# Second gather of a graph kernel: one comparison of 1024 columns for four tiles' one-hots, followed by four additions, in place of one comparison per tile

## What is computed

```python
def _L1_gnn_ref(x, edge_index, W1, b1, W2, b2, gamma, beta):
    src, dst = (edge_index[0], edge_index[1])
    msg_sum = jax.ops.segment_sum(x[src], dst, num_segments=N)
    cnt = jax.ops.segment_sum(jnp.ones_like(dst, dtype=x.dtype), dst, num_segments=N)
    local_mean = msg_sum / jnp.maximum(cnt, 1.0)[:, None]
    feature_diff = jnp.tanh(jnp.linalg.norm(x - local_mean, axis=1, keepdims=True))
    enhanced = jax.nn.relu(x @ W1 + b1) @ W2 + b2
    h = x + ALPHA * enhanced * feature_diff
    ...
x = _layernorm(x + _L0_gnn_ref(...), axis=-1)
x = _layernorm(x + _L1_gnn_ref(x, edge_index, ...), axis=-1)
```

## Time and profile before

| | |
|---|---|
| median of 3 runs | 3951.27 us (3940.12 to 3954.78) |
| the profiled execution | 3949.06 us, its span 3947.3 us |
| busy over the span | PE 77%, DVE 75%, POOL 68%, ACT 56% |
| second gather, first product to last addition | 3044.0 to 3868.3 us |
| line 1461, DVE comparisons | 880, mean 361 ns |
| line 1453, DVE additions | 880, mean 424 ns |
| line 1258, POOL gathers of direct groups | 608, mean 959 ns |

### The profile page before, as it was taken

How to read it: one execution, slowest core, us unless ns; L and a number is a source line. 1 busy time by engine, 2 the same in 40 slices (tenths; PEclk the granted TensorE clock), 3 DMA queues, 4 the chain that set the end, 5 groups by cost and what they waited for, 6 DMA issues and landing times. The chain is left out here.

```text
span 3947.3 us, 81199 instructions
## 1 busy us (share of the span) xinstructions
PE 3027.4 (77%) x17192; PEld 2107.0 (53%) x17193; DVE 2949.3 (75%) x7793; ACT 2222.9 (56%) x6111; POOL 2695.6 (68%) x2634
## 2 busy tenths in 40 slices
PE   6865888888888999999999966767774477666652
PEld 2321444444436777777777745556663355455541
DVE  8998899989985555455454538999996589778857
ACT  1422999999985666666666659989993000000003
POOL 3887777777776777777777740048888777777770
PEclk8976999999999999999999987888887788888876
DMA  7332333333335888888888894457763222222232
GB/s 202 117 101 88 105 97 104 98 104 100 102 98 176 263 261 263 261 260 262 263 259 263 261 243 177 186 209 274 267 241 121 86 74 79 79 78 78 73 50 38
DMA packets 314706, 637.18 MB, mean 161 GB/s; under 512 B 54382, under 2 KB 188567, under 8 KB 306551
## 3 DMA queue, kind: packets, MB, share of 16 engines
q0 software_dynamic: 99440, 246.26, 22.6%
q1 hardware_dynamic: 172984, 266.56, 21.0%
q10 hardware_dynamic: 42192, 123.38, 8.3%
HBM read 423.94 MB, written 212.05 MB: 161 GB/s over the span
## 5 line engine op out<-in xcount | busy, mean ns | idle before, releaser
L367 POOL DMA_INDIRECT rec_d<-arena x830 | 886.0, 1068 | 311.2 <-issue 310.9
L853 POOL DMA_INDIRECT arena<-b_tab,arena x880 | 838.6, 953 | 292.1 <-issue 257.9
L767 PE MATMUL psum<-arena 128*128 128x440 f16 x3360 | 675.7, 356 | 34.9 <-ACT arena L461 33.3
L874 DVE TENSOR_TENSOR arena<-psum,arena 128x512 f32<-128x512 f32 x440 | 284.6, 686 | 551.5 <-DMA arena<-b_tab,arena 310.2
L964 PE MATMUL psum<-weT,arena 128*128 128x256 f32 x1760 | 548.7, 394 | 55.7 <-DVE arena L874 52.1
L461 ACT ACTIVATE arena<-arena 128x128 f16<-128x128 f16 x1680 | 561.7, 386 | 0.0
L626 DVE TENSOR_SCALAR arena<-iota_t,arena 128x880 f16<-128x880 f16 x840 | 500.8, 661 | 51.9 <-PE psum L767 49.3
L767 PEld LDWEIGHTS psum<-arena 128*128 128x128 f16 x3360 | 323.5, 99 | 381.9 <-DVE arena L626 56.3
L1453 DVE TENSOR_TENSOR arena<-psum,arena 128x256 f32 x880 | 372.9, 424 | 156.9 <-PE psum L1573 150.1
L1573 PE MATMUL psum<-x_sb,arena 128*128 128x256 f32 x1152 | 320.9, 439 | 198.7 <-DVE x_sb L1461 85.3
L967 PE MATMUL psum<-arena 128*128 x2640 | 435.1, 274 | 0.0
(11 more groups left out here) (255 smaller groups left out, 5807.2 us busy)
## 6 DMA issues: line engine op xcount, KB each, us to landing
z_d<-arena ACTq DMA_DIRECT2D x220, 512.0 KB
arena<-z_d SPq DMA_DIRECT2D x44, 2560.0 KB
arena<-rec_d SPq DMA_DIRECT2D x220, 260.0 KB
arena<-in_edge_attr SPq DMA_DIRECT2D x83, 640.0 KB, 4.8
arena<-early_d SPq DMA_DIRECT2D x34, 512.0 KB
arena<-b_tab,arena POOLq DMA_INDIRECT x880
rec_d<-arena POOLq DMA_INDIRECT x831, 3.4
early_d<-arena POOLq DMA_DIRECT2D x9, 1024.0 KB, 4.2
```

The source lines that it names most:

```text
L367: nc.gpsimd.indirect_dma_start(rec_rows, bass.IndirectOffsetOnAxis(e_idx[:, s, k:k + 1], 0), e_buf[:, s, k, :], None).then_inc(s_es[s], 16)
L767: last = nc.tensor.matmul(bank(4 + 2 * k + h)[:, 0:HALF], hot_lane[:, s, k, :], hot_tile[:, s, h * HALF:(h + 1) * HALF], start=start, stop ...
L853: nc.gpsimd.indirect_dma_start(bg[:, s, k, :], None, b_tab, bass.IndirectOffsetOnAxis(rec[:, s, k, H:H + 1].bitcast(I32), 0)).then_inc(s_b ...
```

## The change

The eight comparisons of 256 columns of a turn become two of 1024 columns, a `tensor_tensor` instead of a `tensor_scalar`. The ramp is repeated over four tiles, and the four columns of `l1_loc` are each repeated over 256 columns. The first stands ahead of additions 0 to 3, the second ahead of additions 4 to 7.

```diff
+        HOTS_IN_ONE = 4
...
                     wait(dve, s_sg, 8 * u - 8)
                     for k in range(G):
-                        t = first_tile(kind, n) + k
-                        last = nc.vector.tensor_scalar(hotg[:, place % 2, k, :], iota256[:], l1_loc[:, bass.ds(t, 1)], None, ALU.is_equal)
+                        if k % HOTS_IN_ONE == 0:
+                            t = first_tile(kind, n) + k
+                            wanted = l1_loc[:, bass.ds(t, HOTS_IN_ONE)].unsqueeze(2).broadcast_to([P, HOTS_IN_ONE, Z])
+                            last = nc.vector.tensor_tensor(hotg[:, place % 2, k:k + HOTS_IN_ONE, :], iota256[:].unsqueeze(1).broadcast_to([P, HOTS_IN_ONE, Z]),
+                                                           wanted, ALU.is_equal)
+                            if k + HOTS_IN_ONE == G:
+                                last.then_inc(s_hg, 1)
                         if before is not None:
-                            if k == G - 1:
-                                last.then_inc(s_hg, 1)
                             pair_add(*before[0:2], k, pairs[k])
-                    if before is None:
-                        last.then_inc(s_hg, 1)
```

## The result

The changed kernel takes 4049.35 us (median of 4 runs, 4046.95 to 4051.69) against 3945.69 us (4 runs, 3939.13 to 3954.78): 1.0254 times as long, with a 95% interval of 1.0238 to 1.027. That is 104 us slower by the medians; 4057 us was forecast. The profiled execution took 4049.35 us.

The account below looks back on a forecast made before the run. POOL's gathers were taken to bound the kernel, 20.3 us per three turns. Gathers held by the new comparisons add 108 us, VectorE's longer turn not added: 3949 + 108 = 4057 us; range 3998 to 4115, own range 4030 to 4085.

Parts of the forecast that it names:

- The comparison's price: VectorE's new 1024-column comparison: 1.22 us each, with the fifth addition starting 1.48 us after the fourth.
- rival 2: The new comparison's repeated operand reads slowly, up to 2.46 us each; 300 us at that bound, 4153 us halfway; chance 0.12.
- The comparison was free before: In VectorE's turns, the old short comparison filled a gap between additions 0.65 us apart, so its 318 us cost nothing.
- Gathers are held and set the pace: POOL's line 1258 gathers starting during a two-SBUF-input comparison are held until 0.83 us after it; mean 0.96 to 1.13 us.
- By chance: Hold on POOL's gathers priced by random hits: 0.45 us for each of 212 comparisons, 95 us.
- by alignment: Hold on POOL's gathers priced by where holding places later ones: 72 us loop, 36 unrolled, 7 last eight turns; together 115.
- the 108 us: The loss taken for held gathers over the whole kernel, chosen between 95 and 115 us, nearer to the latter.
- VectorE alone would pass POOL: Three unheld VectorE turns take 22.6 us in the loop and 21.6 before it, against the gathers' 20.3 us.
- rival 1: Gathers are not held by the comparison, so VectorE's turns bound: net 53 us, 4002 us, up to 4015; chance 0.18.
- One signature: VectorE's wait for products was to fall from 148 us to some tens.

Follow-up runs that it names:

- half additions: The changed kernel with additions of 128 instead of 256 columns, leaving half of each product out of the sums: 1.0183 against the kernel before, 71 us over.
- the kernel with the new order and no hold: The changed kernel with four one-input comparisons of 256 columns in a row, then four additions: 1.018 against the kernel before, 67 us over.
- the kernel with the longest comparisons: The changed kernel with one comparison of 2048 columns for a whole turn: 5367.86 us beside 5570.79 us of the kernel before, ratio 0.9659, slow transfers.
- the kernel before with half additions: The kernel before with additions of 128 columns, half of each product left out: 5340.42 us beside 5498.03 us of the kernel before, slow transfers.

## Why the prediction was right

**The comparison's price** (1.22 us, 1.48 us between fourth and fifth addition) was right: 1.220 and 1.48. The repeated second operand costs nothing, so rival 2 is out. The rule on adjacent words that the Trainium skill ("Vector Engine (DVE) Microarchitecture Reference", the SBUF access granule) states would have given an estimated 1.9 us, and the 1.220 us show that it does not apply to this repeated word.

**The comparison was free before.** Right: with 49 us less of it no time came back, and additions without a comparison between them still start 0.65 us apart; 86.3 us of the gaps are put down to the addition before.

**Gathers are held and set the pace.** Right: mean 1.13 us as forecast, idle time unchanged, last gather at 3950.4 instead of the forecast 3958. By chance I had 95 us and by alignment 115 for the hold; it is 105.7, between the two. Part by part the alignment was the better account: it gave 36 us for the unrolled turns, 72 for the loop and 7 for the last eight turns, and the gathers' time over 0.952 us each is 37.9, 70.6 and 1.7 us there (the kernel before has 1.8, 2.6 and 0.1). The held gathers in the timeline above, 0.90 and 0.32 us over, are the 0.9 and 0.3 us of that working. The size is still no constant of the comparison: with half additions the same comparisons cost 64 us, because VectorE's turn brings them to other gathers. That the 108 us came so near to 105.7 is in part luck, since they were chosen between two sums.

**VectorE alone would pass POOL.** Right in kind, a little small in size: rival 1's arithmetic gave 53 to 66 us, and the kernel with the new order and no hold costs 67 us by the medians and 72 by the gathers' sum. Its unrolled turns take 36 us longer than before, as reckoned (37); the loop 55 instead of 46, since a turn takes 7.68 us and not 7.5; and the last eight turns are 23 us shorter instead of 30. So VectorE's turn alone costs 72 us, the hold alone 64 us (with half additions, where it meets other gathers), and both together 106 us rather than 136. As forecast they are not added: in the changed kernel the gathers wait for no slot, so VectorE's longer turn is hidden behind them.

**One signature was wrong.** I expected VectorE's wait for products to fall from 148 us to some tens; the profile has 153.9 us. Two things were left out. The first is how the profile names a wait. Of the 153.9 us, 44.7 us are 201 waits of 0.22 us, the gap that stands between two additions anyway (the earlier trace rows has one of 0.22 us put down to PE and one put down to DVE); now that no comparison fills these gaps, the additions show them. The second is that the gathers impose waits at both ends that the change can't touch: one wait of 38.1 us for the first direct group (42.8 us before), and 40 us in the last eight turns, in which VectorE waits for each group (42 us before). In the 60 turns of the loop the waits longer than 0.24 us did fall, from 31.1 to 20.6 us. The stretch from 3350 to 3750 us shows it, the kernel before first:

```profile
L1453 DVE TENSOR_TENSOR arena<-psum,arena 128x256 f32 x477 | 202.2, 424 | 39.5 <-PE psum L1573 35.7 <-issue 0.3
...
L1454 DVE TENSOR_TENSOR arena<-psum,arena 128x256 f32 x412 | 174.3, 423 | 78.4 <-DVE arena L1454 40.7 <-PE psum L1575 37.7
```

Of the 35.7 us, 28.7 are waits over 0.24 us; of the 37.7 us, 14.6. In the same stretch PE ran at a lower granted clock (columns as in the earlier trace rows):

```profile
3350.00:3750.00 400.00, 272.83 (x832) 197.20 (x832) 290.18 (x530) 8.83 (x47) 317.53 (x271) 0.79 0.24 67
```

PE has 832 records of products where it had 952, yet is busy for 273 us instead of 265: the granted clock is 0.79 instead of 0.88, so PE spent more of the stretch at the lower of its two levels (1.2 GHz). What lowered the clock was not tested. It cost no time that these traces show: in the changed kernel the gathers set the pace, and in the loop of the kernel with four short comparisons (granted clock 0.84) VectorE's waits for products over 0.24 us come to 0.8 us in all.

## What to carry to other kernels

Before merging small operations of an engine, look whether they fill a wait that stays: a chain of additions that each wait for the one before has room for a short comparison between them and none for a long one. And when GpSimd's indirect transfers set the pace, count every VectorE operation with two SBUF inputs that runs beside them as theirs: a first estimate of the loss is the chance that a gather starts during it times what is then left of it. Here that gave 95 us, and alignment made it 106 in the changed kernel and 64 with half additions. One input in PSUM, or a one-input operation of the same work, avoids it.

None of the kernels that ran beside the kernel before at 3963.51 us beats it.

## What the hardware showed that was not expected

- A comparison of 1024 columns takes 1.22 us with both inputs in SBUF and with the ramp in PSUM alike; the former holds gathers and the latter doesn't.
- Short one-input comparisons in a row, 1.2 us together, don't hold a gather (0.957 us for the 147 that started during them), though nine of them kept one held after a two-input operation had caught it (8.29 us in the earlier trace rows).
- With slow transfers the kernel with the longest comparisons was 3.4% faster than the kernel before (0.9659), and the medians of all the other kernels there lie 1.8 to 4.0% under that of the kernel before too. The gathers of the first waited 4.0 + 2.7 us for slots, where those of the kernel before with half additions waited 122.4 + 169.7 us. The cause was not followed up, and no trace of the kernel before with slow transfers was kept.
